# V of all heads made in the recurrent stage and kept in HBM, its splits on GpSimd, and the attention loop reordered

## The chip, the cores and the metric

The kernel runs on one core of a Trainium2 chip. The metric is device time in microseconds (us) from the first to the last instruction of one execution; lower is better. The core's engines each run their own queue of instructions in order and wait for one another through semaphores: TensorE (PE in the profile, PEld its weight loads), VectorE (DVE), ScalarE (ACT), GpSimd (POOL), and SyncE (SP), whose queue issues most of the transfers.

## What is computed

A GRU runs over 128 time steps of 16 sequences with 256 features; its output is added to `x`. A transformer block follows on 16 sequences of 128 tokens, with 16 heads of 128 and a conditioning vector per sequence. Cut to what matters here:

```python
x = x + gru(cond, x, W_ih, W_hh, b_ih, b_hh)          # 128 steps, one after the other
shift1, scale1, gate1, shift2, scale2, gate2 = split(cond @ ada_w + ada_b, 6)
x1 = layernorm(x) * (1 + scale1) + shift1
q, k, v = split(x1 @ qkv_w + qkv_b)                    # 16 heads of 128
p = softmax(q @ k.T / sqrt(128))
x = x + gate1 * ((p @ v) @ out_w + out_b)
x2 = layernorm(x) * (1 + scale2) + shift2
x = x + gate2 * (gelu(x2 @ ffn_w1 + ffn_b1) @ ffn_w2 + ffn_b2)
```

## The kernel before, in words

Products of float32 values are made of float16 halves: a value is split into a high half (a rounded copy) and a low half (value minus high half), and three matmuls, high by high, low by high and high by low, add up in PSUM (`product`, lines 428 to 430). Splitting a value therefore takes one copy (most on ScalarE) and one subtraction (most on VectorE).

The kernel has three stages.

*The recurrence.* 16 blocks (r) of 8 time steps (s). In a step TensorE multiplies the state with the gate weights (`gru_step`, lines 535 and 543), ScalarE and VectorE make the gates in turn, and a scan on VectorE (line 1210) makes the next state, for which the next step's matmuls wait. In TensorE's queue, behind the step's last gate matmuls, stands filler: the input products of the next block (`x_products`), the turn and normalisation of the rows of the block before (`rows_T`, `rows_back`), which gives y = x1 for 8 more tokens of all 16 sequences, and `ahead(item)`: q and k of the four heads 0, 6, 8, 14 (`AHEAD`), for all sequences, a block of 8 tokens at a time, kept on the chip as `qk_hi`, `qk_lo`. ScalarE also splits the weights, four pieces of 320 columns a block (`piece_high`, line 901), and GpSimd their low halves (line 347).

*Attention.* 64 head steps d: four groups g of four sequences, 16 heads each. In a step the kernel makes q and k of the head unless it is one of the four (`queries`, `keys`, 6 matmuls of 512 columns each), V of the head (`values`, 24 matmuls of 128 columns), the scores (`scores`, 12 of 128), the row maximum on VectorE (line 1282), four exponentials on ScalarE (line 996), the normalisation on VectorE (line 1299, counted by `s_pn`), the high half of p on ScalarE (`prob_high`, line 989, `p_h`), the low half on VectorE (`prob_low`, line 1293, `p_l`), two transposing transfers issued by SyncE (`turn`, line 307, `p_turn`), p times V (`attend`, 12 of 128) and the output projection (`project_out`, 6 of 512). The order of the work is written out by hand for each engine. On TensorE a step d is keys(d), values(d), project_out(d-3), attend(d-2), queries(d+1), scores(d). There is one buffer each of p, its halves and their transposes. At the end of a group GpSimd makes sums and low halves of the second normalisation (lines 378, 387, 393, 400), each behind the maximum of a given head (`behind_max`).

*Feed-forward.* 32 tiles (`up`, `down`) for the four groups, and the output.

Of the kernel before, what the change touches and what calls it, by code (L numbers as in the profile page):

```python
# [15 lines left out]
P = 128  # L16
# [23 lines left out]
QKV_PIECES = -(-3 * INNER * KD // PC)  # L40

HEADS = NG * H
AHEAD = (0, 6, 8, 14)
NA = len(AHEAD)
ITEMS = [(e, n, 1, 0, B, 4, 2 * P) for n in range(NBL - 2) for e in range(NA)]
LAST_ITEMS = {"old": (0, NBL - 2, 1, 0, B, 2, 0), "new": (0, NBL - 1, 1, 0, QUAD, 3, 0), 1: (1, NBL - 2, 2, 0, B, 5, 0),
              "rest": (0, NBL - 1, 1, QUAD, B, 4, 0), 2: (2, NBL - 2, 2, 0, B, 4, 0), 3: (3, NBL - 2, 2, 0, B, 4, 0)}
LAST = {what: len(ITEMS) + i for i, what in enumerate(LAST_ITEMS)}
ITEMS += LAST_ITEMS.values()
WHOLE = [d for d in range(HEADS) if d % H not in AHEAD]  # L50
SLOTS = [(which, head) for head in AHEAD for which in range(2)]
SLOTS += [(which, head) for which in range(3) for head in range(H) if (which, head) not in SLOTS]
AHEAD_PIECES = -(-2 * NA * KD * DH // PC)
LAG = 3
# [5 lines left out]
FORWARD, BACK, HIGH = {4: 0, 6: 1}, {11: 0, 12: 1}, {12: 0, 14: 1}  # L60
ROW_TILES = {3: (0, 0), 4: (0, 1), 5: (1, 0), 6: (1, 1)}
STATS, CENTRE, MODULATE = {6: 0, 8: 1}, {10: 0, 11: 1}, {12: 0, 14: 1}
VAR = 9
LATER = {4: "rest", 6: 2, 9: 3}
REST_AT, SUM_AT, LOW_AT = 5, 11, 15

AHEAD_PLACE = {0: 0, 2: 1, 4: 2, 6: 3}
# [13 lines left out]
def build(nc, x, cols_in, cond_rows, gate_rows, W_ih, W_hh, ada_a, ada_r, ada_b, weights, out):  # L81
# [3 lines left out]
    with ctx:  # L85
# [15 lines left out]
        y_hi = sb("y_hi", [P, KD, B, T], f16)  # L101
        y_lo = sb("y_lo", [P, KD, B, T], f16)
        qk_hi = sb("qk_hi", [P, NA, 2, B, T], f16)
        qk_lo = sb("qk_lo", [P, NA, 2, B, T], f16)
# [50 lines left out]
        v_hi = sb("v_hi", [P, 3, N], f16)  # L155
        v_lo = sb("v_lo", [P, 3, N], f16)
        pT_hi = sb("pT_hi", [P, QUAD, T], f16)
        pT_lo = sb("pT_lo", [P, QUAD, T], f16)
        aT_hi = sb("aT_hi", [P, 2, N], f16)
        aT_lo = sb("aT_lo", [P, 2, N], f16)  # L160
        prob = sb("prob", [P, QUAD, T])
        p_hi = sb("p_hi", [P, N], f16)
        p_lo = sb("p_lo", [P, N], f16)
        mx = sb("mx", [P, QUAD])
        nmx = sb("nmx", [P, QUAD])
        den = sb("den", [P, QUAD])
        rden = sb("rden", [P, QUAD])
        four = sb("four", [P, 4, N], f16)
# [7 lines left out]
        gated = xn[:, :, :].rearrange("p j d -> p (j d)").rearrange("p (k j t) -> p k j t", k=KD, j=QUAD)  # L176
        qT_hi, qT_lo, kT_hi, kT_lo = (four[:, i, :] for i in range(4))
        hid_hi, hid_lo = four[:, 0:2, :], four[:, 2:4, :]
# [14 lines left out]
        def sems(names):  # L193
# [15 lines left out]
        xt_hi, xt_lo, xp_lo, qk_mm, qk_h, qk_l = sems("xt_hi xt_lo xp_lo qk_mm qk_h qk_l")  # L209
# [3 lines left out]
        (ln_ag, ln_nat, ln_T, ln_st, ln_ve, ln_rstd, ln_xn, ln_B, ln_y, ln_hi, ln_lo) = sems(  # L213
            "ln_ag ln_nat ln_T ln_st ln_ve ln_rstd ln_xn ln_B ln_y ln_hi ln_lo")
        (q_mm, k_mm, v_mm, s_mm, a_mm, o_mm, q_h, k_h, v_h, q_l, k_l, v_l, s_mx, s_nm, s_exp, s_rd, s_pn,
         p_h, p_l, p_turn, a_h, a_l, o_gated, o_res) = sems(
             "q_mm k_mm v_mm s_mm a_mm o_mm q_h k_h v_h q_l k_l v_l s_mx s_nm s_exp s_rd s_pn "
             "p_h p_l p_turn a_h a_l o_gated o_res")
# [16 lines left out]
        flat_prob = prob[:, :, :].rearrange("p j t -> p (j t)")  # L235

        def ahead_place(item, part):

            e, n, blocks, b0, b1, at, col = ITEMS[item]
            width = blocks * BS * (b1 - b0)  # L240
            ps = bank[at][:, col + part * width:col + (part + 1) * width].rearrange("p (b t) -> p b t", b=b1 - b0)
            return ps, slice(b0, b1), slice(n * BS, (n + blocks) * BS)

        def a_late(d):

            return d < HEADS - 1 and (d % H in AHEAD or (d + 1) % H in AHEAD)

        def whole_before(d):

            return sum(w < d for w in WHOLE)  # L250

        def tall_bank(d, which):

            return bank[which + (6 if d == WHOLE[1] else 0)]

# [4 lines left out]
        def up_bank(t):  # L260
            return bank[(0, 1, 4, 2)[t] if t < 4 else 1 + t % 2]

# [4 lines left out]
        def _(sp):  # L267
# [17 lines left out]

            for r in range(NBL - 1):
# [22 lines left out]
            for d in range(HEADS):  # L309
                turn(d)  # L310
# [1165 lines left out]
```

## Time and profile before

| | |
|---|---|
| time, median of 3 runs | 753.85 us (753.35 to 753.98) |
| span of the profiled execution | 754.3 us |
| mean granted TensorE clock, share of 2.4 GHz | 0.988 |
| TensorE busy | 724.2 us (96%) |
| VectorE, ScalarE, GpSimd busy | 580.0, 488.7, 104.7 us |
| recurrence, to the last scan | 0 to 267.8 us |
| first score maximum, last score maximum | 274.9, 660.4 us |
| end | 754.3 us |

A row of the profile names a line of the kernel, the engine, the operation, the output and inputs by the program's names (L1299 DVE prob<-prob,rden is the normalisation in line 1299), shapes as partitions x elements, and times. The views used are the page (busy time, chain of waits, transfers), the busy time in stretches, the instructions of one line with shortest, median and longest duration, and the instructions in order of time. Matmul ends are modelled, so the distance from start to start is the rate.

### The profile page before, as it was taken

What the parts mean: (1) busy time and instruction counts of PE and PEld (TensorE: products, weight loads), DVE (VectorE), ACT (ScalarE), POOL (GpSimd) and SP (SyncE); (2) the same over time, 40 slices, a digit from 0 to 9 for tenths busy, and PEclk for the clock granted to TensorE, in tenths of its full rate; (3) what the DMA queues carried; (4) which work ended last, traced back from release to release, by engine and by line L of the source; (5) the groups of instructions that cost most, each with busy time, mean ns of one, the idle gap of its engine ahead of it and who ended that gap; (6) DMA issues with size and microseconds to landing.
All of it is one profiled execution on the core that took longest, in us unless ns stands there. A gap on an engine that the chain in (4) does not pass through costs nothing.

```text
span 754.3 us, 25863 instructions
## 1 busy us (share of the span) xinstructions
PE 724.2 (96%) x10644; PEld 534.1 (71%) x10644; DVE 580.0 (77%) x1625; ACT 488.7 (65%) x1665; POOL 104.7 (14%) x134
## 2 busy tenths in 40 slices
PE   6899999999999989999999999999999999999997
PEld 5688888888888766767667677676676766644554
DVE  5778877888888877777778888788887888834643
ACT  4456555665565566677777677777678777766453
POOL 0322222223232210000001011010110101000040
PEclk9899998999999999999999999999999999999999
DMA  6311121111121002222222312222222231310001
GB/s 234 102 45 45 46 69 63 45 46 44 46 62 55 3 16 43 44 43 42 46 43 43 50 37 56 38 50 44 44 43 43 43 49 37 48 25 28 29 1 56
DMA packets 77869, 36.75 MB, mean 49 GB/s; under 512 B 70539, under 2 KB 73783, under 8 KB 77751
## 3 DMA queue, kind: packets, MB, share of 16 engines
q1 hardware_dynamic: 77175, 33.52, 19.5%
q8 instruction: 84, 1.38, 0.7%
q10 hardware_dynamic: 576, 1.57, 0.6%
q14 instruction: 34, 0.28, 0.1%
HBM read 16.20 MB, written 2.10 MB: 24 GB/s over the span
## 4 chain that ended last, share of the span: by engine, by line
PE 83%; DVE 6%; DMA 4%; ACT 3%; issue 2%; SPq 2%; DVEq 0%; POOL 0%; POOLq 0%
PE bank L428 20%; PE bank L430 19%; PE bank L429 19%; PE bank L535 12%; PE bank L543 5%; PE bank L448 4%; DMA pT_lo<-p_lo 3%; DVE h_hi L1210 2%; SPq L307 2%; ACT zg L936 1%; DVE nu L1204 1%; PE bank L435 1%; PE bank L464 1%; PE bank L457 1%; DMA x<-in_x 0%
## 5 line engine op out<-in xcount | busy, mean ns | idle before, releaser
L428 PE MATMUL bank<-y_hi,w_hi 128*128 128x512 f16 (+2 forms) x496 | 140.6, 301 | 0.3 <-DVE qk_lo L1187 0.2
L430 PE MATMUL bank<-y_lo,w_hi 128*128 128x512 f16 (+2 forms) x496 | 140.8, 302 | 0.0
L429 PE MATMUL bank<-y_hi,w_lo 128*128 128x512 f16 (+2 forms) x496 | 140.7, 302 | 0.0
L535 PE MATMUL bank<-h_hi,whh_hi 128*128 128x16 f16 x1536 | 110.9, 173 | 14.1 <-DVE h_hi L1210 11.7
L535 PEld LDWEIGHTS bank<-h_hi,whh_hi 128*128 128x128 f16 x1536 | 89.5, 96 | 36.7 <-DVE h_hi L1210 34.5
L996 ACT ACTIVATE prob<-bank,nmx 128x128 f32<-128x128 f32 x256 | 90.4, 366 | 29.7 <-DVE nmx L1285 29.7
L535 PE MATMUL bank<-h_hi,whh_lo 128*128 128x16 f16 x1536 | 108.7, 172 | 0.0
L535 PEld LDWEIGHTS bank<-h_hi,whh_lo 128*128 128x128 f16 x1536 | 90.0, 96 | 0.1
L428 PE MATMUL bank<-w_hi,y_hi 128*128 128x128 f16 x512 | 89.1, 219 | 0.5 <-DVE v_lo L1289 0.5
L429 PE MATMUL bank<-w_hi,y_lo 128*128 128x128 f16 x512 | 89.1, 219 | 0.0
L430 PE MATMUL bank<-w_lo,y_hi 128*128 128x128 f16 x512 | 89.1, 219 | 0.0
L543 PE MATMUL bank<-h_lo,whh_hi 128*128 128x16 f16 x1536 | 77.6, 172 | 0.1
L347 POOL TENSOR_TENSOR w_lo<-stage,w_hi 128x320 f16<-128x320 f32 x64 | 52.2, 816 | 143.1 <-DVE h_lo L1215 141.1
L430 PEld LDWEIGHTS bank<-y_lo,w_hi 128*128 128x128 f16 x496 | 48.9, 99 | 29.4
L934 ACT ACTIVATE zr<-bank 128x32 f32<-128x32 f32 x128 | 25.6, 200 | 58.6 <-PE bank L543 55.2
L428 PEld LDWEIGHTS bank<-y_hi,w_hi 128*128 128x128 f16 x496 | 48.8, 98 | 19.6 <-issue 0.5
L429 PEld LDWEIGHTS bank<-y_hi,w_lo 128*128 128x128 f16 x496 | 48.8, 99 | 17.5
L989 ACT ACTIVATE p_hi<-prob 128x512 f16<-128x512 f32 x64 | 40.5, 632 | 30.5 <-DVE prob L1299 19.5
L1282 DVE TENSOR_REDUCE mx<-bank 128x4 f32<-128x512 f32 x64 | 44.1, 689 | 18.3 <-PE bank L430 17.8
L1326 DVE TENSOR_TENSOR four<-nat,four 128x512 f16<-128x512 f32 (+1 forms) x33 | 22.7, 689 | 44.8 <-ACT four L1032 44.7
L543 PEld LDWEIGHTS bank<-h_lo,whh_hi 128*128 128x128 f16 x1536 | 56.3, 96 | 0.2 <-DVE h_lo L1215 0.2
L912 ACT ACTIVATE qk_hi<-bank,small 128x128 f16<-128x128 f32 (+3 forms) x124 | 39.1, 367 | 26.4 <-PE bank L430 26.4
(156 smaller groups left out, 2161.6 us busy)
## 6 DMA issues: line engine op xcount, KB each, us to landing
stage<-in_weights SPq DMA_DIRECT2D x16, 640.0 KB, 3.9
x<-in_x SPq DMA_DIRECT2D x16, 128.0 KB, 3.8
out<-xr SPq DMA_DIRECT2D x3, 512.0 KB, 3.1
xr<-in_ada_r SPq DMA_DIRECT2D x1, 1024.0 KB, 7.6
pT_hi<-p_hi SPq DMA_TRANSPOSE x64, 2.4
pT_lo<-p_lo SPq DMA_TRANSPOSE x64, 2.5
xr<-in_W_ih ACTq DMA_DIRECT2D x2, 384.0 KB, 3.8
xr<-in_W_hh ACTq DMA_DIRECT2D x2, 384.0 KB, 5.8
```

The costliest lines, as they stand in the source:

```text
L347: gtt(w_lo[:, j * PC:(j + 1) * PC], stage[:, r % 2, i * PC:(i + 1) * PC], w_hi[:, j * PC:(j + 1) * PC], sub).then_inc(piece_lo, 1)
L428: mm(ps, w[0], a[0], start=start, stop=False, skip_group_check=True)
L429: mm(ps, w[1], a[0], start=False, stop=False, skip_group_check=True)
L430: return mm(ps, w[0], a[1], start=False, stop=stop, skip_group_check=True)
L448: nc.tensor.matmul(gate_cols(n, m), w[:, k, m * P:(m + 1) * P], a[:, n % 2, k, :], start=False, stop=False, skip_group_check=True)
L535: nc.tensor.matmul(out(m0 + m), half[:, k, (m0 + m) * P:(m0 + m + 1) * P], h_hi[:, k * B:(k + 1) * B, 1], start=False, stop=False, skip_gr ...
L543: mm = nc.tensor.matmul(out(m0 + m), whh_hi[:, k, (m0 + m) * P:(m0 + m + 1) * P], h_lo[:, k * B:(k + 1) * B], start=False, stop=k == KD - ...
L912: op = nc.scalar.activation(qk_hi[:, e, part, b, t], ps, ident_f, bias=bT[:, at:at + 1])
L934: nc.scalar.activation(zr[:, :, 1], r_cols[r % 2][:, s, :], ACT.Sigmoid).then_inc(r_ok, 1)
L989: nc.scalar.activation(p_hi[:, :], flat_prob, copy).then_inc(p_h, 1)
L996: op = nc.scalar.activation(prob[:, j, :], bank[3][:, j * T:(j + 1) * T], ACT.Exp, bias=nmx[:, j:j + 1], scale=SCALE, accum_out=den[:, j:j ...
L1282: nc.vector.reduce_max(mx[:, :], bank[3][:, :].rearrange("p (j s) -> p j s", j=QUAD), AX.X).then_inc(s_mx, 1)
```

## The change

V of all 16 heads and sequences is made in the recurrence. An item (n, pair) of `VITEMS` multiplies block n of the rows (128 rows: 16 sequences by 8 tokens) with the V weights of two heads: 6 matmuls of 256 columns. `VPLACE` puts 109 of the 128 items behind steps 14 to 127, one a step from step 35 on; 19 (`VTAIL` and up) follow in the tail of the recurrence and among the first three heads. ScalarE copies the items of the recurrence from PSUM, ScalarE and VectorE in turn the others, to `v_rows`; SyncE stores half blocks of 512 KB to `v_spill` in HBM and loads 256 KB a head (`load_values`) into `v_full`. The q and k items ahead and `values` are gone; every head makes q and k in its own step.

In attention GpSimd makes the low half of p, and both halves of V from `v_full`. `prob`, the halves of p, q and k and the transposes have two buffers. TensorE's step is keys(d), project_out(d-4), queries(d+1), attend(d-2), scores(d). GpSimd's loop over heads carries its group-end work too. The second normalisation writes to space in the weight tiles (`x2_hi`, `x2_lo`), and its turns use the two banks of the projection. The diff, cut to its core:

```diff
+LAG = 4
+GATE, RESIDUAL = {4: 0, 6: 1}, {5: 0, 7: 1}
+STATS, CENTRE, MODULATE = {8: 0, 9: 1}, {11: 0, 12: 1}, {13: 0, 14: 1}
+VAR = 10
+REST, SUM, LOW = {9: 0, 10: 1}, {12: 0, 13: 1}, {0: 0, 1: 1}
...
             def turn(d):
                 for half_ok, src, dst in ((p_h, p_hi, pT_hi), (p_l, p_lo, pT_lo)):
                     sp.wait_ge(half_ok, d + 1)
-                    if d > 0:
-                        sp.wait_ge(a_mm, d)
-                    sp.dma_start_transpose(dst[:, :, :], src[:, :]).then_inc(p_turn, 16)
+                    if d > 1:
+                        sp.wait_ge(a_mm, d - 1)
+                    sp.dma_start_transpose(dst[:, d % 2, :, :], src[:, d % 2, :]).then_inc(p_turn[d % 2], 16)
+            def load_values(d):
+                g, head = d // H, d % H
+                if d > 1:
+                    sp.wait_ge(v_l, d - 1)
+                sp.dma_start(v_full[:, d % 2, :].rearrange("p (j c) -> p j c", j=QUAD),
+                             v_spill[:, g * QUAD:(g + 1) * QUAD, head * DH:(head + 1) * DH]).then_inc(v_in[d % 2], 16)
+            for n in (NBL - 2, NBL - 1):
+                sp.wait_ge(v_out[n % 2][0], 16 * (NBL // 2))
+            load_values(0)
+            load_values(1)
+            turn(0)
+            for d in range(1, HEADS):
                 turn(d)
...
+                if d + 1 < HEADS:
+                    load_values(d + 1)
...
-            for g in range(NG - 1):
-                first = (g + 1) * H
-                for k in range(KD):
-                    behind_max(first + REST_AT + k)
-                    bias_rest(g, k)
...
+            def prob_low(d):
+                pool.wait_ge(p_h, d + 1)
+                gtt(p_lo[:, d % 2, :], flat_prob[d % 2], p_hi[:, d % 2, :], sub).then_inc(p_l, 1)
+            def value_split(d):
+                pool.wait_ge(v_in[d % 2], 16 * (d // 2 + 1))
+                if d > 2:
+                    pool.wait_ge(a_mm, d - 2)
+                nc.gpsimd.tensor_copy(v_hi[:, d % 3, :], v_full[:, d % 2, :]).then_inc(v_h, 1)
+                pool.wait_ge(v_h, d + 1)
+                gtt(v_lo[:, d % 3, :], v_full[:, d % 2, :], v_hi[:, d % 3, :], sub).then_inc(v_l, 1)
+            for d in range(HEADS):
+                prob_low(d)
+                if d >= H and (d + 1) % H == VAR:
+                    norm_rstd(d // H - 1)
+                value_split(d)
+                g, i = (d + 2) // H, (d + 2) % H
+                if d + 2 < HEADS:
+                    pool.wait_ge(s_pn, d + 3)
+                if g > 0 and i in REST:
+                    bias_rest(g - 1, REST[i])
+                if g > 0 and i in SUM:
+                    sum_rest(g - 1, SUM[i])
+                if g > 1 and i in LOW:
+                    norm_low(g - 2, LOW[i])
...
+            def value_item(i):
+                n, pair = VITEMS[i]
+                pe.wait_ge(lb_lo, n + 1)
...
+                for k in range(KD):
+                    mm = product(ps, (y_hi[:, k, n, :], y_lo[:, k, n, :]),
+                                 (wq_hi[:, heads, k, :], wq_lo[:, heads, k, :]), k == 0, k == KD - 1)
+                mm.then_inc(v_mm, 1)
...
-            share = (0, 0, 7, 9, 22, 25, 31, 32, 36)
+            share = (0, 0, 2, 9, 16, 23, 27, 33, 36)
...
+                    if t1 - 1 in VPLACE:
+                        value_item(VPLACE[t1 - 1])
...
             def attend(d):
-                pe.wait_ge(p_turn, 32 * (d + 1))
+                pe.wait_ge(p_turn[d % 2], 32 * (d // 2 + 1))
+                pe.wait_ge(v_l, d + 1)
...
+            for d in range(LAG, HEADS):
                 g, i = d // H, d % H
+                keys(d)
+                project_out(d - LAG)
...
+                if d < HEADS - 1:
+                    queries(d + 1)
...
+                attend(d - 2)
                 scores(d)
...
             def softmax(d):
                 act.wait_ge(s_nm, d + 1)
-                if d > 0:
-                    act.wait_ge(p_l, d)
+                if d > 1:
+                    act.wait_ge(p_l, d - 1)
...
+                    if t1 - 1 in VPLACE:
+                        value_out(VPLACE[t1 - 1])
...
+                softmax(d - 1)
+                key_high(d)
                 prob_high(d - 1)
...
+                    query_high(d + 1)
                 attend_high(d - 2)
...
                 score_max(d - 1)
...
+                query_low(d)
+                attend_low(d - 3)
+                softmax(d - 1)
+                key_low(d)
```

(The last two runs of lines are the loops over heads of ScalarE and VectorE.)

## Rows read from the trace of the kernel before

**Rows 1.** The page's chain that ended last: share of the span by engine.
```profile
PE 83%; DVE 6%; DMA 4%; ACT 3%; issue 2%; SPq 2%; DVEq 0%; POOL 0%; POOLq 0%
```
**Rows 2.** Busy time in stretches: stretch, length, busy us of each engine, granted clock, DMA.
```profile
core 0: us, PE busy (x) PEld busy (x) DVE busy (x) ACT busy (x) POOL busy (x), PEclk, DMA share, GB/s
12.00:267.80 255.80, 241.29 (x5951) 210.59 (x5951) 208.88 (x872) 145.34 (x722) 69.15 (x92) 0.97 0.18 57
293.10:660.40 367.30, 364.47 (x3851) 255.44 (x3850) 303.12 (x592) 269.54 (x792) 22.72 (x20) 1.00 0.25 44
```
**Rows 3.** One line, the scan that ends a step: duration, first and last start.
```profile
L1210 DVE TENSOR_TENSOR_SCAN h_hi<-zz,nu x128: 291/292/293, 12.0 to 267.6; 128x64 f16<-128x64 f32 x128
```
**Rows 4.** In order of time, TensorE in one step: start, duration, instruction.
```profile
264.81 0.25 PE L543 MATMUL bank<-h_lo,whh_hi 128*128 128x16 f16 x4
...
265.94 0.18 PE L535 MATMUL bank<-h_hi,whh_hi 128*128 128x16 f16 x1
```
**Rows 5.** In order of time, ScalarE in the same step.
```profile
265.26 0.23 ACT L939 ACTIVATE nu<-npre 128x32 f32<-128x32 f32 x1
...
266.65 0.20 ACT L934 ACTIVATE zr<-bank 128x32 f32<-128x32 f32 x1
```
**Rows 6.** In order of time, TensorE: matmuls of 256 columns back to back.
```profile
276.07 0.27 PE L428 MATMUL bank<-y_hi,w_hi 128*128 128x256 f16 x1
276.18 0.27 PE L429 MATMUL bank<-y_hi,w_lo 128*128 128x256 f16 x1
```
**Rows 7.** In order of time, TensorE: first of 24 narrow matmuls, then two of 512.
```profile
359.14 0.23 PE L428 MATMUL bank<-pT_hi,v_hi 128*128 128x128 f16 x1 [0.24 <-DMA pT_lo<-p_lo]
...
360.49 0.38 PE L428 MATMUL bank<-y_hi,w_hi 128*128 128x512 f16 x1
360.70 0.38 PE L429 MATMUL bank<-y_hi,w_lo 128*128 128x512 f16 x1
```
**Rows 8.** Instructions grouped by form: busy us, mean ns, idle before.
```profile
L901 ACT ACTIVATE w_hi<-stage 128x320 f16<-128x320 f32 x64 | 28.4, 469 | 0.0
```
**Rows 9.** The page's transfers: issuing queue, count, size, us to landing.
```profile
out<-xr SPq DMA_DIRECT2D x3, 512.0 KB, 3.1
```
**Rows 10.** In order of time, VectorE: maxima of heads 3, 14, 63, normalisation of 3.
```profile
293.14 0.68 DVE L1282 TENSOR_REDUCE mx<-bank 128x4 f32<-128x512 f32 x1
...
295.81 0.69 DVE L1299 TENSOR_TENSOR prob<-prob,rden 128x512 f32<-128x512 f32 x1
...
360.69 0.69 DVE L1282 TENSOR_REDUCE mx<-bank 128x4 f32<-128x512 f32 x1 [0.16 <-PE bank L430]
...
660.40 0.69 DVE L1282 TENSOR_REDUCE mx<-bank 128x4 f32<-128x512 f32 x1 [0.35 <-PE bank L430]
```
**Rows 11.** In order of time: an operation on VectorE that releases one on GpSimd.
```profile
399.31 0.17 DVE L1285 TENSOR_SCALAR nmx<-mx 128x4 f32<-128x4 f32 x1
...
399.56 1.04 POOL L393 TENSOR_TENSOR xr<-xr,gb 128x512 f32<-128x512 f32 x1 [126.27 <-DVE nmx L1285]
```
**Rows 12.** Single lines, GpSimd's 512-column operations: shortest, median, longest ns.
```profile
L387 POOL TENSOR_TENSOR y_lo<-xn,y_hi x8: 1154/1158/1164, 459.3 to 723.8; 128x512 f16<-128x512 f32 x8
...
L393 POOL TENSOR_TENSOR xr<-xr,gb x8: 1037/1040/1487, 399.6 to 726.4; 128x512 f32<-128x512 f32 x8
...
L400 POOL TENSOR_TENSOR xr<-xr x8: 1256/1268/1758, 434.7 to 729.1; 128x512 f32<-128x512 f32 x8
```
**Rows 13.** In order of time: a high half of p and the issue of its transpose.
```profile
302.91 0.63 ACT L989 ACTIVATE p_hi<-prob 128x512 f16<-128x512 f32 x1 [0.40 <-DVE prob L1299]
...
303.77 1.19 SPq L307 DMA_TRANSPOSE pT_hi<-p_hi  x1
```
**Rows 14.** In order of time: low transpose, attend's first weight load; landing times.
```profile
356.62 1.22 SPq L307 DMA_TRANSPOSE pT_lo<-p_lo  x1
...
359.13 0.10 PEld L428 LDWEIGHTS bank<-pT_hi,v_hi 128*128 128x128 f16 x1 [0.73 <-DMA pT_lo<-p_lo]
...
DMA to landing us min/median/max: 2.4/2.5/4.2
```
**Rows 15.** Busy time in stretches, the end of the kernel; columns as in rows 2.
```profile
749.00:750.00 1.00, 0.92 (x7) 0.50 (x6) 0.89 (x5) 0.00 (x0) 0.00 (x0) 1.00 0.00 0
...
753.00:754.00 1.00, 0.00 (x0) 0.00 (x0) 0.00 (x0) 0.00 (x0) 0.00 (x0) 0.67 0.43 125
```

More of the change, by code:

```diff
@@ L39, with value_items, by_scalar, taken @@
 GK = 32 + 2 * GM
-QKV_PIECES = -(-3 * INNER * KD // PC)
+TALL_PIECES = -(-(H + 2) * DH * KD // PC)
 HEADS = NG * H
[L43 to L54, printed above, removed]
+PAIRS = H // 2
+VP = 2 * DH
+SIDE = INNER // 2
+SLOTS = [(2, head) for head in range(H)] + [(which, head) for head in range(H) for which in range(2)]
+def value_items():
+    first = [(0, 0), (0, 1), (0, 2), (0, 3), (0, 4), None, None, None, (1, 0), (1, 1), (0, 5), (1, 2), (1, 3),
+             (0, 6), None, None, (0, 7), (1, 4), (1, 5), (1, 6), (1, 7)]
+    order, place = [], {}
+    for i, item in enumerate(first):
+        if item:
+            place[BS + 6 + i] = len(order)
+            order.append(item)
+    at = BS + 6 + len(first)
+    for n in range(2, NBL - 2):
+        for pair in range(PAIRS):
+            if at < T:
+                place[at] = len(order)
+                at += 1
+            order.append((n, pair))
+    order += [(NBL - 2, pair) for pair in range(PAIRS // 2)] + [(NBL - 1, pair) for pair in range(PAIRS // 2)]
+    order += [(NBL - 2, pair) for pair in range(PAIRS // 2, PAIRS)]
+    order += [(NBL - 1, pair) for pair in range(PAIRS // 2, PAIRS)]
+    return order, place
+VITEMS, VPLACE = value_items()
+VTAIL = len(VPLACE)
+def by_scalar(i):
+    return i < VTAIL or i % 2 == 0
+def taken(i):
+    scalar = sum(by_scalar(j) for j in range(i + 1))
+    return scalar, i + 1 - scalar
+def piece_of(pair):
+    return -(-(pair + 1) * VP * KD // PC)
+LAG = 4
 TILES = NG * FM
@@ L154, in build @@
         xn = sb("xn", [P, QUAD, D])
[L155 to L168, printed above, removed]
+        gated = sb("gated", [P, KD, QUAD, T])
+        hid_hi = sb("hid_hi", [P, 2, N], f16)
+        hid_lo = sb("hid_lo", [P, 2, N], f16)
+        v_spill = nc.dram_tensor("v_spill", (T, B, INNER), f32).ap()
         bank = [ctx.enter_context(nc.psum_tensor(f"bank{i}", [P, 512], f32)) for i in range(8)]
@@ L800, in last_down @@
                     mm.then_inc(f_down, 1)
[L802 to L804 removed]
+            for which, ready in ((0, q_mm), (1, k_mm)):
+                if which == 0:
+                    pe.wait_ge(lb_lo, NBL)
+                tall_parts(tall_rest, 0, which, last).then_inc(ready, 1)
+            tall_parts(tall_rest, 1, 1, before)
+            tall_parts(tall_rest, 1, 0, last).then_inc(q_mm, 1)
+            tall_parts(tall_rest, 1, 1, last).then_inc(k_mm, 1)
+            for i in range(VTAIL + 5, VTAIL + 7):
+                value_item(i)
             scores(0)
[L806 to L807 removed]
+            for i in range(VTAIL + 7, VTAIL + 11):
+                value_item(i)
+            pe.wait_ge(piece_lo, NBL * PB)
+            queries(2)
             scores(1)
[L809 to L811 removed]
+            value_item(VTAIL + 11)
+            value_item(VTAIL + 12)
+            keys(2)
+            value_item(VTAIL + 13)
+            value_item(VTAIL + 14)
             queries(3)
```

557 lines of the change are left out of this document (233 added, 324 removed).

## The prediction

> **What bounds the kernel now.** I read the chain that ended last first: TensorE carries 83% of it [rows 1]. An average over stages says little, so the second view is the busy time by stage [rows 2]. From 293.1 to 660.4 us, the 60 head steps between the score maxima of heads 3 and 63, TensorE is busy for 364.5 of 367.3 us: there attention runs at the rate of its matmuls. In the recurrence (12.0 to 267.8 us) it is busy for 241 of 256 us, but the third view, the 128 scans that end the steps, shows another limit [rows 3]: 127 intervals in 255.6 us, 2.01 us each, 1.96 us wherever the clock is full. In one such step [rows 4] the last gate matmuls start at 264.81, and the next step's first matmul at 265.94 begins only when the scan has ended; the matmuls between are filler of no weight while they fit. Four 25 ns matmuls after 264.81 leave a window of about 1.02 us. ScalarE has such a window too [rows 5]: its tanh ends at 265.49, the next gate is due at 266.65.
>
> **The change: the recurrence.** Removed are 56 items of q and k ahead, each 12 matmuls of 128 columns; added are 109 items of V, one a step from step 35 on, each 6 matmuls of 256 columns. At 0.11 us from start to start [rows 6] an item takes 0.65 us. With the gate products of the next block, up to 7 matmuls of about 0.056 us (24 narrow matmuls in 1.35 us [rows 7]), a step's filler is 1.04 us: just at the window's edge. At s = 1, where the bias matmul lies too (1,024 columns, some 0.45 us), it is over by about 0.2. ScalarE has more to lose. The V copy can start only when the item's last matmul is through (264.92 + 0.65 + 0.2 = 265.8) and takes about 0.37 us, 256/320 of the 0.469 us of a weight piece [rows 8]; until 266.65 there is then room for one piece. At s = 3 there are two: over by 0.45 us. At s = 7 a modulation tile and a piece: over by 0.15 in eight rounds. Some 14 x 0.45 + 12 x 0.2 + 8 x 0.15 = 10 us; VectorE drops a 0.34 us operation a step, and the steps beyond 1.96 us (6.7 us in all [rows 3]) may be fewer with more columns in TensorE. I take **+8**, bounds -6 (nothing late, no slow step) and +22.
>
> **Between the stages.** 19 items of V remain for the tail. Eleven of them (7 us of TensorE) stand before the second query product; five before the last rows are turned or the first scores. The start of head 0 comes about 3 us later. Then attend(0) needs V back from HBM: the eleventh item is copied after the softmax of head 0, stored (512 KB landed in 3.1 us [rows 9]), loaded (256 KB in 512-byte pieces; I take 4 us, no transfer like it is here; 2 to 6), split on GpSimd (about 2.5 us, below). That is some 4 us after TensorE could start it, of which the queue's work behind it hides nothing. **+7** at head 3, bounds 0 and +12.
>
> **Attention, the matmuls.** V's 24 matmuls leave; per head remain 24 of 128 columns (1.35 us) and 18 of 512 (0.215 each [rows 7], 3.87): 5.22 us, where a head now takes 367.3 / 60 = 6.12 on the mean. If TensorE stayed the limit, 60 heads would take 313 us, 54 us less. VectorE loses two operations a head, ScalarE one. What is decisive is what attend waits for.
>
> **Attention, the new wait.** GpSimd's loop over heads now does prob_low(d), value_split(d), and then, for every d, waits for s_pn >= d + 3. s_pn counts the normalisations on VectorE, so this is softmax(d+2). Queued behind it is prob_low(d+1). So the low half of head d+1 is made only after the softmax of head d+2, although its own high half has been ready for a whole head. On TensorE the order is keys(d+3), project_out, queries(d+4), attend(d+1), scores(d+3): attend(d+1) needs that low half transposed. Scores(d+2) -> softmax(d+2) -> prob_low(d+1) -> transpose -> attend(d+1) -> scores(d+3) is thus a closed loop that advances one head. Its length, from one score maximum to the next:
> - maximum to end of the normalisation: 293.14 to 295.81 + 0.69 = 3.36 us [rows 10]. Two VectorE splits stand beside the exponentials in it, as they do now.
> - hand-over to GpSimd: 0.08 us [rows 11].
> - prob_low on GpSimd, 128x512, f16 from f32 and f16: 1.16 us, the row of the same form [rows 12] (other forms 1.04 and 1.27). It was 0.69 us on VectorE.
> - to the queue: 0.23 us, end of p_hi at 303.54 to the issue at 303.77 [rows 13].
> - issue of the low transpose to attend's first weight load: 356.62 to 359.13, 2.51 us [rows 14]. Landing takes 2.4 us at least, 2.5 in the middle and 4.2 at most, where it follows the high half's closely. Here the high half goes out a head earlier, so 2.5.
> - attend and scores to the next maximum: 359.13 to 360.69, 1.56 us [rows 10, 14].
>
> Sum **8.90 us a head**. TensorE's other work between, three products of 1.29 us, fills 3.87 of the 7.34 us before attend: it idles for about 3.5 us a head. v_l stays inside: cast and subtraction follow prob_low. The trace has no 512-column cast on GpSimd; it costs between nothing and the 1.16 us of the subtraction, which reads two inputs where the cast reads one. Even at the upper end 1.16 + 1.16 + 0.2 = 2.5 us is under the 2.74 us of queue and transpose, so either value adds nothing. The load of V is asked for a head earlier, behind the low transpose, and has 8.9 us. GpSimd's other work sits between the wait and prob_low, so it lengthens the loop: in the 16 heads with such an operation 6 x 1.04 + 6 x 1.27 + 4 x 1.16 = 18 us [rows 12]. The four-row transposes and the norm's VectorE work fall in the idle time. 60 x 8.90 + 18 = 552 us, against 367.3 [rows 10]: **+185**. Bounds: 8.5 us a head (shorter hand-overs) gives +161; 9.2 (the transpose at 2.8) +203.
>
> A row bears on prob_low's price: its sibling forms have 1.04 and 1.27 us as medians but 1.49 and 1.76 at most [rows 12], and the slow ones ran in the last stage, beside a VectorE subtraction of two SBUF tensors. The Trainium skill (GPSIMD Engine Reference, Key points) says that GpSimd shares its SBUF interfaces with VectorE and contends with VectorE instructions that have two SBUF inputs. By that rule the new wait does good, as it keeps GpSimd away from the normalisation; were prob_low hit all the same, the sum would be 0.45 x 60 = 27 us more.
>
> **The clock.** At the end of the kernel the last matmul is over at 749.9 and the granted clock falls from 2.4 to 1.2 GHz within 753 to 754 (mean 0.67 [rows 15]), so about 3.4 us later. It also fell for parts of the recurrence (mean 0.97 [rows 2]), where TensorE was busy but with narrow matmuls. [...] The three products have slack at half speed; attend and scores have not: up to 24 x 0.056 = 1.35 us a head, 0 to +80 us. A half-speed product shortens the next gap, so it can't happen everywhere at will: I take **+25**, a third.
>
> **The end.** One more project_out follows the last scores (+1.3), and attend(62) stands in the same loop with three products before it: 7.34 - 3.87 = +3.5. Together **+5**. Feed-forward is the same.
>
> **How the numbers follow.** 754.3 + 8 + 7 + 185 + 25 + 5 = 984; the profiled span is 0.4 us above the median of the runs, so **984 us**. The range goes from 754.3 - 6 + 0 + 161 + 0 + 5 = 914 to 754.3 + 15 + 12 + 203 + 80 + 5 = 1069; the ends need all terms on one side, so 920 to 1060.
>
> **Rivals.**
> - The loop isn't closed, attention stays at the rate of its matmuls. If prob_low(d) waited only for its own high half, the chain to attend would be 3.36 + 0.7 (p_hi, 0.63 [rows 13], and its hand-over) + 1.16 + 0.23 + 2.51 = 8.0 us, and TensorE's work between scores(d) and attend(d) is 5.22 + 3.87 = 9.1: it would be hidden. Then 754.3 + 8 + 7 - 54 + 1 = **716 us**, faster. It decides at one point: whether s_pn can reach d + 3 before the scores of head d + 2. I find no second place that counts it up. Chance 0.05.
> - The clock is at 1.2 GHz in every attend: 8.90 + 1.35 = 10.25 us a head, 984 - 25 + 80 = **1039 us**. [...] Against: after each gap 5.2 us of dense matmuls. Chance 0.15.
> - GpSimd runs beside VectorE's two-input operations after all: +27, **1011 us**. Chance 0.08.
> - Forecast 0.7; 0.02 for the loop shorter than 8.5 us.
>
> A measurement of this kernel can tell 0.2% from no change. Faster 0.05, same 0.01, slower 0.94.
>
> **What would show it.** Right: from head 3 on score maxima about 8.9 us apart, TensorE idle for 3 to 3.5 us before attend with the low transpose as releaser, GpSimd's prob_low(d+1) released by the normalisation of head d+2, and steps of 10 us where GpSimd has a norm operation. The recurrence ends 8 us later, with gates late at s = 3. Wrong: maxima 5.2 us apart, or prob_low released by p_hi; steps far over 2.1 us in the recurrence; v_l or the load of V as attend's releaser; a granted clock that stays at 1.0 or at 0.5 in attention.

## The result and the profile after

The changed kernel takes **994.73 us** in the median of four runs (991.13 to 1000.12), against 753.91 before: a ratio of 1.3194, interval [1.3148, 1.324]. It is 32% slower. The profiled execution took 991.13 us, with a span of 989.3 us.

The page's chain that ended last, the share of the span by engine, answers to [rows 1]:

```profile
issue 39%; PE 35%; POOL 20%; DVE 2%; DMA 2%; ACT 1%; SPq 0%; POOLq 0%; DVEq 0%
```

Before, TensorE carried 83% of the chain. Now it carries 35%; a fifth is GpSimd, and 39% is time for which the view finds no releaser. The busy time in stretches answers to [rows 2] and has its columns: the recurrence, the start of attention, the 60 head steps between the score maxima of heads 3 and 63, and the end.

```profile
12.00:280.30 268.30, 260.80 (x5921) 233.75 (x5921) 181.89 (x761) 151.20 (x718) 69.12 (x92) 0.97 0.36 105
280.30:314.00 33.70, 28.27 (x271) 20.74 (x270) 18.04 (x44) 18.88 (x52) 7.12 (x8) 0.99 0.41 102
314.00:889.30 575.30, 405.63 (x2569) 231.87 (x2568) 259.17 (x501) 256.08 (x749) 194.11 (x199) 0.86 0.27 57
889.30:989.30 100.00, 92.18 (x490) 47.28 (x488) 43.25 (x99) 51.35 (x90) 17.47 (x15) 0.98 0.09 28
```

In the third stretch TensorE was busy for 364.5 of 367.3 us; now it is busy for 405.6 of 575.3, with fewer matmuls and at a granted clock of 0.86 in place of 1.00. That stretch holds 208 of the 235 us by which the span grew. By the same four marks in both traces (last scan, maximum of head 3, maximum of head 63, end):

| us | before | after | difference | predicted |
|---|---|---|---|---|
| to the last scan | 267.55 | 280.06 | +12.5 | +8 |
| from there to the maximum of head 3 | 25.59 | 33.97 | +8.4 | +7 |
| heads 3 to 63 | 367.26 | 575.28 | +208.0 | +210 (185 + 25 for the clock) |
| from there to the end | 93.9 | 100.0 | +6.1 | +5 |

The waits, the engine and operation, what it waited for, us in total, times, longest:

```profile
DVE mx L1319 <- PE bank L527: 293.3, 63, 7.0
POOL p_lo L487 <- DVE prob L1328: 285.7, 46, 7.0
PEld bank L525 <- DMA pT_lo<-p_lo: 208.2, 63, 4.9
```

These three are the closed loop that the prediction describes: the maximum waits for the scores, GpSimd's low half of p waits for a normalisation, attend waits for the transposed low half. One turn of it in order of time, from one score maximum to the next (start, duration, instruction):

```profile
607.15 0.69 DVE L1319 TENSOR_REDUCE mx<-bank 128x4 f32<-128x512 f32 x1 [6.92 <-PE bank L527]
...
609.83 0.69 DVE L1328 TENSOR_TENSOR prob<-prob,rden 128x512 f32<-128x512 f32 x1
...
610.60 1.16 POOL L487 TENSOR_TENSOR p_lo<-prob,p_hi 128x512 f16<-128x512 f32 x1 [6.90 <-DVE prob L1328]
...
611.78 1.19 SPq L373 DMA_TRANSPOSE pT_lo<-p_lo  x1
...
614.27 0.10 PEld L525 LDWEIGHTS bank<-pT_hi,v_hi 128*128 128x128 f16 x1 [2.23 <-DMA pT_lo<-p_lo]
...
615.82 0.69 DVE L1319 TENSOR_REDUCE mx<-bank 128x4 f32<-128x512 f32 x1 [4.64 <-PE bank L527]
```

Every link has its row: 3.37 us from the maximum to the end of the normalisation (610.52), 0.08 to GpSimd, 1.18 for p_lo and the queue, 2.49 from the issue of the transpose to attend's first weight load, 1.55 for attend and scores. That is 8.67 us, and undisturbed heads are 8.62 to 8.70 us apart all through the stage. The mean is 9.59; the rest is heads with a norm operation and heads in which the clock fell (the run with the idle time filled tells the two apart). A fall of the clock can be seen in the distance of two matmuls of 512 columns, 0.22 us at 2.4 GHz and 0.43 us at 1.2 GHz (the granted clock from 624.6 to 626.0 us is 0.50):

```profile
610.42 0.38 PE L525 MATMUL bank<-aT_hi,w_hi 128*128 128x512 f16 x1
...
610.64 0.38 PE L526 MATMUL bank<-aT_hi,w_lo 128*128 128x512 f16 x1
...
624.73 0.63 PE L525 MATMUL bank<-y_hi,w_hi 128*128 128x512 f16 x1
625.16 0.63 PE L526 MATMUL bank<-y_hi,w_lo 128*128 128x512 f16 x1
```

### The profile page after: what moved, and what is told of

Same layout as the page of the kernel before. It is cut to its first block, busy times and chain, and to the rows that moved or that the text cites. A ratio compares the mean times of both kernels' runs of the same rounds, so it can differ in the third digit from the quotient of the medians.

```text
span 989.3 us, 23647 instructions
## 1 busy us (share of the span) xinstructions
PE 793.4 (80%) x9324; PEld 539.1 (54%) x9324; DVE 508.3 (51%) x1423; ACT 483.5 (49%) x1621; POOL 289.5 (29%) x326
## 4 chain that ended last, share of the span: by engine, by line
issue 39%; PE 35%; POOL 20%; DVE 2%; DMA 2%; ACT 1%; SPq 0%; POOLq 0%; DVEq 0%
PE bank L630 8%; POOL p_lo L487 7%; POOL v_lo L496 7%; PE bank L525 6%; PE bank L527 5%; PE bank L526 5%; PE bank L545 4%; PE bank L638 4%; POOL v_hi L494 3%; DMA pT_lo<-p_lo 1%; POOL xr L482 1%; PE bank L532 1%; DVE h_hi L1249 1%; POOL xr L475 1%; PE bank L597 1%
## 5 line engine op out<-in xcount | busy, mean ns | idle before, releaser
L525 PE MATMUL bank<-pT_hi,v_hi 128*128 128x128 f16 x256 | 57.1, 250 | 177.7 <-DMA pT_lo<-p_lo 177.7
L487 POOL TENSOR_TENSOR p_lo<-prob,p_hi 128x512 f16<-128x512 f32 x64 | 74.1, 1157 | 294.1 <-DVE prob L1328 285.7
L525 PE MATMUL bank<-y_hi,w_hi 128*128 128x512 f16 x248 | 111.9, 451 | 0.0
L526 PE MATMUL bank<-y_hi,w_lo 128*128 128x512 f16 x248 | 109.5, 441 | 0.0
L527 PE MATMUL bank<-y_lo,w_hi 128*128 128x512 f16 x248 | 107.3, 433 | 0.0
L496 POOL TENSOR_TENSOR v_lo<-v_full,v_hi 128x512 f16<-128x512 f32 x64 | 74.5, 1165 | 5.1
L525 PE MATMUL bank<-w_hi,y_hi 128*128 128x256 f16 x256 | 69.6, 272 | 0.7 <-DVE v_rows L1228 0.4
L527 PE MATMUL bank<-w_lo,y_hi 128*128 128x256 f16 x256 | 69.9, 273 | 0.0
L526 PE MATMUL bank<-w_hi,y_lo 128*128 128x256 f16 x256 | 69.8, 273 | 0.0
L527 PE MATMUL bank<-four 128*128 128x128 f16 x256 | 66.0, 274 | 0.0
L526 PE MATMUL bank<-four 128*128 128x128 f16 x256 | 65.3, 272 | 0.0
```

Source lines behind the costliest of these rows:

```text
L487: gtt(p_lo[:, d % 2, :], flat_prob[d % 2], p_hi[:, d % 2, :], sub).then_inc(p_l, 1)
L496: gtt(v_lo[:, d % 3, :], v_full[:, d % 2, :], v_hi[:, d % 3, :], sub).then_inc(v_l, 1)
L525: mm(ps, w[0], a[0], start=start, stop=False, skip_group_check=True)
L526: mm(ps, w[1], a[0], start=False, stop=False, skip_group_check=True)
L527: return mm(ps, w[0], a[1], start=False, stop=stop, skip_group_check=True)
```

## The experiments

Eight kernels were run. All start from the changed kernel or from an experiment on it; ratios are to the kernel before, measured in the same series.

### The wait taken away

```diff
-                if d + 2 < HEADS:
-                    pool.wait_ge(s_pn, d + 3)
```

> The changed kernel without GpSimd's wait for s_pn >= d + 3; nothing else differs. Closed loop (the wait sets 8.7 us a head, the rest is the clock and GpSimd's norm work): the low half of head d+1 then follows its own high half, the chain to attend (about 8.0 us) fits in the 9.1 us that TensorE needs from scores to attend, and the score maxima come 5.2 to 5.4 us apart: 60 x 5.3 = 318 us in place of 575, granted clock near 1.0, total 725 to 740 us. Rival (GpSimd as such: 2.9 us of splits a head with three operations in a row, or V's way through HBM, sets the pace): maxima stay above 7 us apart, total above 840 us.

Measured: **750.94 us**, ratio 0.9964 [0.9948, 0.9979]. The wait is the cause of the loss: without it 244 us go, and the stretch from head 3 to head 63 takes 342.0 us in place of 575.3. But the stretch does not come down to the rate of its matmuls (313 us), and the time lies between what the two theories gave: where GpSimd has no norm operation, most heads are 5.22 and 5.97 us apart in turn. The order of time of VectorE and GpSimd shows what the slower ones have. The negated maximum `nmx`, four elements a partition, takes 0.17 us in 33 of the 60 heads, more than 1 us in 25 and 0.44 and 0.55 us in two:

```profile
493.76 0.17 DVE L1320 TENSOR_SCALAR nmx<-mx 128x4 f32<-128x4 f32 x1
...
493.93 1.16 POOL L496 TENSOR_TENSOR v_lo<-v_full,v_hi 128x512 f16<-128x512 f32 x1
...
498.94 1.15 POOL L496 TENSOR_TENSOR v_lo<-v_full,v_hi 128x512 f16<-128x512 f32 x1
...
498.99 1.13 DVE L1320 TENSOR_SCALAR nmx<-mx 128x4 f32<-128x4 f32 x1
```

In the first head `nmx` starts 0.17 us ahead of `v_lo` and takes its 0.17. In the second it starts 0.05 behind `v_lo` and ends at 500.12, just behind `v_lo`'s end at 500.09. In each of the 27 heads in which `nmx` is longer than 0.17 us, it ends 0.02 to 0.03 us behind the end of a GpSimd operation (`v_lo`, once `v_hi`). All exponentials, and with them the whole chain, wait for `nmx`. Whether the meeting is the cause or a coincidence was left to the next run.

### The wait taken away, and v_lo begun behind the maximum

On top of the edit above:

```diff
                 pool.wait_ge(v_h, d + 1)
+                if d + 1 < HEADS:
+                    pool.wait_ge(s_nm, d + 2)
                 gtt(v_lo[:, d % 3, :], v_full[:, d % 2, :], v_hi[:, d % 3, :], sub).then_inc(v_l, 1)
```

> The edit of e1_no_wait (GpSimd's wait for the normalisation taken away) and one more: GpSimd begins the subtraction that makes v_lo(d) only when VectorE has made nmx(d+1), so that v_lo can no longer run beside that small operation. In e1_no_wait every second nmx met v_lo and took 1.09 to 1.13 us in place of 0.17, and the maxima were alternately 5.22 and 5.97 us apart (342 us from head 3 to head 63, span 750.1). If it is the meeting with GpSimd that stretches nmx, nmx is 0.17 in every head, the maxima are 5.2 to 5.4 us apart, heads 3 to 63 take 315 to 325 us and the kernel 722 to 736 us, under both kernels. If the meeting is a coincidence and something else sets the second interval, or if the waiting GpSimd is late with p_lo, the time stays at 745 us or more.

Measured: **735.4 us** (735.34 to 736.65), ratio 0.9724 [0.97, 0.9747]: 2.8% faster than the kernel before, and 259 us faster than the change as it was made. One line of each trace, VectorE's `nmx` in attention (count, busy us, mean ns, idle before), first in the experiment above:

```profile
L1320 DVE TENSOR_SCALAR nmx<-mx 128x4 f32<-128x4 f32 x60 | 34.7, 579 | 2.0
```

and in this one:

```profile
L1322 DVE TENSOR_SCALAR nmx<-mx 128x4 f32<-128x4 f32 x60 | 10.2, 170 | 2.0
```

The busy time of this kernel in attention, with the columns of [rows 2]:

```profile
313.00:638.00 325.00, 321.54 (x2560) 190.76 (x2558) 260.39 (x501) 243.17 (x748) 194.48 (x198) 1.00 0.46 100
```

The `nmx` is 0.17 us in every head, 24.5 us of busy time are gone, and heads 3 to 63 take 325.7 us where they took 342.0. So it was the meeting with GpSimd. TensorE is busy for 321.5 of 325.0 us at a granted clock of 1.00: attention runs close to its matmuls' rate, 26 of the 60 heads 5.21 to 5.24 us apart. The Trainium skill (SBUF — State Buffer, section "SBUF: two separate sides") says that VectorE and GpSimd share a port pair as an exclusive lock, and that, between a GpSimd operation and a VectorE operation that has two SBUF inputs or runs in a mode with two ports, whichever starts first holds the pair for its whole length while the other blocks. These rows agree with the lock: the one that came 0.05 us later waited for the other's end. `nmx` has one SBUF input; that it runs in such a mode is shown by no run here.

### Scores ahead of attend, the wait kept

```diff
                     pe.wait_ge(q_l, HEADS)
                     up(0)
-                attend(d - 2)
                 scores(d)
+                attend(d - 2)
```

(This is the loop over heads from 4 on; at head 3 the order stays attend, then scores.)

> The changed kernel with the wait kept, but scores(d) issued before attend(d-2) in TensorE's loop. Closed loop: scores(d+3) then no longer stands behind attend(d+1), so the loop scores(d+2), softmax(d+2), prob_low(d+1), transpose, attend(d+1), scores(d+4) advances two heads in about 7.2 + 0.7 + 3.9 + 0.7 = 12.5 us: 6.2 to 6.7 us a head, 60 heads in 375 to 420 us with GpSimd's norm work, total 790 to 840 us. Rival (the wait itself is harmless, some resource takes 8.7 us a head: GpSimd, the transposes, the clock): the order doesn't matter, total stays within 2% of 991 us.

Measured: **918.17 us**, ratio 1.217 [1.2136, 1.2203]. Neither theory: the order matters, but heads are still 8.3 us apart in the mean. In order of time, GpSimd, VectorE, TensorE and ScalarE:

```profile
353.69 1.15 POOL L496 TENSOR_TENSOR v_lo<-v_full,v_hi 128x512 f16<-128x512 f32 x1
...
354.18 0.69 DVE L1322 TENSOR_SCALAR nmx<-mx 128x4 f32<-128x4 f32 x1
...
355.54 0.23 PE L525 MATMUL bank<-pT_hi,v_hi 128*128 128x128 f16 x1 [2.12 <-DMA pT_lo<-p_lo]
...
356.42 0.69 ACT L1067 ACTIVATE aT_hi<-bank,small 128x512 f16<-128x512 f32 x1 [3.05 <-PE bank L527]
357.00 0.36 ACT L1047 ACTIVATE prob<-bank,nmx 128x128 f32<-128x128 f32 x1
```

The scores' negated maximum is ready at 354.87 (`nmx` met `v_lo` here too and took 0.69 us), but the exponentials start at 357.00, for ahead of them in ScalarE's queue stands the copy of an attend (`aT_hi`), which waits for that attend, which waits for its transposed low half. The loop had been opened on TensorE and was closed again one engine further on.

### The same, and the copies of attend one head later

On top of the edit above, ScalarE copies attend(d-3) in place of attend(d-2) at step d, and VectorE does its part behind the normalisation:

```diff
-                attend_high(d - 2)
+                attend_high(d - 3)
...
-                attend_low(d - 3)
                 softmax(d - 1)
                 key_low(d)
+                attend_low(d - 3)
```

> The edit of e3_scores_first (scores(d) before attend(d-2), GpSimd's wait kept; 918.17 us, maxima 8.3 us apart in the mean) and one more: the two copies of an attend out of its bank go one head later, ScalarE's behind the exponentials and p_hi of head d-1, VectorE's behind the normalisation of head d-1. My reading of e3_scores_first is that its loop was closed again through the in-order queues, because the exponentials of head d+3 stood on ScalarE behind the copy of attend(d+1). If that is so, the loop now goes on by two heads a turn: a turn of 8.7 to 9.9 us plus scores of 1.6 us, 5.2 to 6.2 us a head, with GpSimd's wait itself still there: heads 3 to 63 take 330 to 400 us and the kernel 745 to 820 us. If the copies were not what closed it, it stays at 900 us or more.

Measured: **891.02 us**, ratio 1.1781 [1.1748, 1.1814]. Over 745 to 820, so the size was missed; heads are 6.95 us apart where nothing disturbs them and 7.9 in the mean. The loop does now advance two heads a turn, as expected. But I had counted too little in a turn:

```profile
353.18 0.68 DVE L1319 TENSOR_REDUCE mx<-bank 128x4 f32<-128x512 f32 x1
...
355.85 0.69 DVE L1328 TENSOR_TENSOR prob<-prob,rden 128x512 f32<-128x512 f32 x1
...
356.62 1.16 POOL L487 TENSOR_TENSOR p_lo<-prob,p_hi 128x512 f16<-128x512 f32 x1 [4.00 <-DVE prob L1328]
...
357.81 1.19 SPq L373 DMA_TRANSPOSE pT_lo<-p_lo  x1
...
360.37 0.22 PE L525 MATMUL bank<-pT_hi,v_hi 128*128 128x128 f16 x1 [1.56 <-DMA pT_lo<-p_lo]
...
364.92 0.22 PE L525 MATMUL bank<-four 128*128 128x128 f16 x1
...
366.42 0.75 DVE L1343 SCALAR_TENSOR_TENSOR aT_lo<-bank,small,aT_hi 128x512 f16<-128x512 f32 x1 [2.26 <-ACT aT_hi L1067]
367.08 0.68 DVE L1319 TENSOR_REDUCE mx<-bank 128x4 f32<-128x512 f32 x1
```

Between attend (360.37) and the scores that come behind it (364.92) now lie the three products of a head, 3.9 us that were outside the loop before; and the maximum (367.08) stands on VectorE behind `aT_lo`, which waits for its high half, 1.3 us after the scores' end. The turn from the maximum at 353.18 to the one at 367.08, two heads on, is 3.36 us to the end of the normalisation, 0.08, 1.19 to the issue of the transpose, 2.56 to attend, 4.55 to the scores and 2.16 to the maximum. These 13.9 us for two heads are 6.95 a head. The wait keeps some loop closed in the two other orders that I tried; of the kernels run here, only those without it are free of it.

### The idle time filled with matmuls

In attention TensorE makes the product queries(d+1) three times; nothing waits for the copies, which overwrite one another.

```diff
-                for k in range(KD):
+                for k in list(range(KD)) * (3 if which == 0 and LAG < d < HEADS else 1):
```

> The changed kernel with the product of queries(d+1) done three times over in TensorE's loop (the first two results are overwritten with the same values): 2.6 us more matmuls a head, in the time in which TensorE idles before attend. If the falls of the granted clock cost what they seem to (maxima 9.59 apart on the mean where undisturbed ones are 8.66 apart), the clock stays near 1.0 and the heads take 8.66 plus GpSimd's norm work: 60 x 8.66 + 18 = 538 in place of 575 us, total 950 to 960 us, less time for more work. If the clock is not what lengthens them, or the idle time was not free: 991 us or more.

Measured: **959.51 us**, ratio 1.2725 [1.2689, 1.2761]: 35 us less with 12 more matmuls of 512 columns in nearly each head. The stretch from head 3 to head 63:

```profile
316.50:860.40 543.90, 485.28 (x3278) 258.73 (x3277) 259.12 (x502) 255.58 (x749) 194.10 (x199) 0.99 0.26 61
```

The granted clock is 0.99 in place of 0.86, and the stretch takes 543.9 us in place of 575.3. So the falls of the clock cost 31.4 us of attention. The matmuls of attend and scores, which have no slack, bear this out: in the changed kernel 16 of 60 attends and 28 of 60 scores run wholly at the lower clock, 0.104 to 0.107 us from start to start in place of 0.056, and others in part, which adds up to 33 us; with the idle time filled it is 2 us. What remains is the loop, 60 x 8.66 = 519.6 us, and 24.3 us more, of which these 2 us are the clock's and the rest lies in the heads with norm operations.

### One matmul of V in place of six

```diff
                 n, pair = VITEMS[i]
...
+                if i < VTAIL:
+                    mm = nc.tensor.matmul(ps, y_hi[:, 0, n, :], wq_hi[:, heads, 0, :], start=True, stop=True,
+                                          skip_group_check=True)
```

(and the six left out for these items)

> The changed kernel with five of the six matmuls of each V item in the recurrence left out (V is incomplete; copies, stores, loads and waits stay). If TensorE's filler is what makes the recurrence later (mean step 2.11 against 1.96 us): every step at 1.96 to 1.98 us, the last scan 10 to 13 us earlier, total 975 to 985 us. If ScalarE's copies and weight pieces are (the +0.45 us at s = 3 of the prediction): the steps stay near 2.11 us, total within 3 us of 991.

Measured: 988.09 us, ratio 1.3107, over the 975 to 985 expected. The last scan starts at 270.88, 9.2 us earlier than in the changed kernel, somewhat under the 10 to 13 expected. The recurrence in stretches:

```profile
12.00:270.90 258.90, 234.80 (x5414) 194.20 (x5411) 182.00 (x762) 140.24 (x722) 68.94 (x92) 0.82 0.38 110
```

ScalarE's copies, VectorE's work and the stores are all still there, so their number is not what lengthens the steps. But a copy can also start earlier when its item has one matmul, so this run alone does not tell TensorE's lateness from ScalarE's; the starts of the next step's first matmul do, and they are given below with the prediction. The granted clock is 0.82 where it was 0.97, and fourteen steps from the second round on took 2.2 to 2.7 us, at a granted clock of 0.50 to 0.79: V also gave TensorE the work that kept its clock up. Heads 3 to 63 took 579.9 us, 4.6 more; that says nothing, for in the two runs below, with the same attention, they took 578.9 and 577.0.

### The order of the input products

Which matmuls are late is told apart by moving them. The steps of a round in the changed kernel are 1.96 us long in the median, except those behind s = 1 (2.31), s = 3 (2.05), s = 5 (2.20), s = 6 (2.21) and, with a modulation tile, s = 7 (2.25).

```diff
-            products = [(m, k, i) for m in range(GM) for k in range(KD) for i in range(3)]
+            products = [(m, k, i) for m in (4, 5, 0, 1, 2, 3) for k in range(KD) for i in range(3)]
```

> The changed kernel with the input products of a round made in another order: those of the n gate (twelve of 36, 0.107 us each in the trace of the changed kernel, the others 0.056) come first, so they fall into the steps s = 2 and 3 in place of s = 5, 6 and 7; nothing else moves. If it is their pace that makes TensorE late in s = 6 (filler of 0.65 for V + 6 x 0.107 against some 1.02 us of room), the step after s = 6 loses its 0.24 us and is like a step without lateness (1.95 to 2.0 us), the steps after s = 2 and s = 3 become 0.3 to 0.4 us longer, and the last scan of the recurrence starts at 279 to 284 us (changed kernel 280.06). If it is ScalarE's evictions or the loads of those steps, the steps after s = 5, 6 and 7 stay as they are and those after s = 2 and 3 too.

Measured: the lateness moved with the products. Behind s = 1, 2, 3, 5 and 6 the steps are 2.42, 2.32, 2.11, 2.04 and 1.96 us long; the last scan starts at 281.29 (one run, span 996.8 us). The sum stays, as expected; the step behind s = 3 grew by 0.06 us only and not by the 0.3 to 0.4 expected, for just three of the twelve products fall there (seven in s = 2, two in s = 1). In s = 2 seven of the n gate's products stand behind V's; TensorE, in order of time:

```profile
237.73 0.32 PE L545 MATMUL bank<-xb_hi,wih_lo 128*128 128x128 f16 x1
237.84 0.31 PE L545 MATMUL bank<-xb_lo,wih_hi 128*128 128x128 f16 x1
```

They are 0.11 us apart, where the products of the other gates are 0.056 apart at the same clock.

### The n gate's products into adjacent columns

The n gate keeps its two parts in one PSUM bank with their columns alternating, so a product writes 16 columns two apart. Here it writes 16 adjacent ones, and the gate no longer finds its sums where it reads them:

```diff
-                return (r_cols[n % 2][:, :, c], z_cols[n % 2][:, :, c], n_cols[n % 2][:, :, c, 1])[m // 2]
+                n_flat = n_bank[n % 2][:, :].rearrange("p (t j) -> p t j", t=BS)
+                return (r_cols[n % 2][:, :, c], z_cols[n % 2][:, :, c], n_flat[:, :, c])[m // 2]
```

> The changed kernel, in which the input products of the n gate go to 16 adjacent PSUM columns a time step in place of 16 columns two apart (the columns are the wrong ones for the gate, so this kernel's recurrence computes something else; its instructions, their count and their shapes stay). If the two-column stride is what makes these twelve products of a round 0.107 us each in place of 0.056, they come down to 0.056, the lateness behind s = 6 and s = 7 goes (2.20 and 1.97 to 2.25 us to 1.96 to 2.1) and that behind s = 5 shrinks (2.20 to about 2.05), and the last scan starts at 271 to 275 us (changed kernel 280.06); the kernel takes 982 to 992 us. If it is the n gate's weights, or the bank, and not the stride, the products stay at 0.107 us and the last scan at 279 us or later.

Measured: 989.55 us (989.09 to 994.74), ratio 1.3098; the last scan starts at 275.16, at the edge of what was expected. The products of an s = 6, in order of time:

```profile
224.19 0.22 PE L546 MATMUL bank<-xb_hi,wih_hi 128*128 128x128 f16 x1
...
224.41 0.22 PE L546 MATMUL bank<-xb_hi,wih_lo 128*128 128x128 f16 x1
224.47 0.22 PE L546 MATMUL bank<-xb_lo,wih_hi 128*128 128x128 f16 x1
```

They come 0.05 to 0.06 us apart, and the next is the first matmul of the following step (224.57). The steps behind s = 5 and 6 are 2.04 and 1.96 us. So the stride of two in the written columns is the cause, not the n gate's weights and not its bank. The order of the computation needs the alternating columns (one scan reads both parts in turn), so this kernel shows the price alone; it leaves out the right sums of the gate.

## Why the prediction was right, and where a step of it failed

The forecast was 984 us (920 to 1060); the profiled execution took 991.13 and the median is 994.73. By its steps:

**The new wait and the closed loop: right.** Mechanism, place and price: 8.90 us a head were forecast, 8.62 to 8.70 are what undisturbed heads take. Against the parts of the sum only one was mis-sized: from the start of p_lo to the issue of its transpose it took 1.18 us and not 1.16 + 0.23; the 0.23 us were an issue behind ScalarE [rows 13], and SyncE was at once there behind GpSimd. The transpose (2.49 against 2.51 [rows 14]), attend and scores (1.55 against 1.56) and the normalisation (3.37 against 3.36 [rows 10]) held. The whole difference hung on one line, and the run without it shows that.

**GpSimd's other operations in the loop: somewhat small.** 18 us were forecast from the operations' durations [rows 12]; with the idle time filled the heads take 24.3 us more than the loop, some 22 of them in heads with norm work. I didn't divide the difference of 4 to 6 us.

**The clock: right in kind, a little small.** +25 was taken as a third of the way to the upper bound, and for the third no row stood; the run with filled idle time gives 31.4 us in attention. The price was put where it fell, on attend and scores. Before attend TensorE idles 1.5 to 4.5 us, 2.8 in the median, where some 3.5 were forecast. The rival with the lower clock in every attend (1039 us) did not come: 33 of 60 attends ran wholly at 2.4 GHz. The two terms above and this one err in opposite directions: 60 x (8.66 - 8.90) = -14, +6 and +6, so that attention as a whole came out at +208.0 against +210. The precise agreement of that row is luck in part.

**Between the stages and the end: right.** The first score maximum comes 3.8 us later behind the last scan (forecast 3) and head 3's another 4.6 us later (forecast 4). The load of V, for which no row stood, lands in 2.9 us (I took 4), the store in 3.8 where the row taken for it had 3.1 [rows 9]. The end is +6.1 against +5.

**The recurrence: the sum near, the reason mostly wrong.** +12.5 against +8, within its bounds. The step that failed is "ScalarE has more to lose". At s = 3, with two weight pieces, I expected 0.45 us; the step behind it is 0.09 us over 1.96. VectorE's scan, ScalarE and the first matmul behind the scan, in order of time:

```profile
238.44 0.29 DVE L1249 TENSOR_TENSOR_SCAN h_hi<-zz,nu 128x64 f16<-128x64 f32 x1
...
238.60 0.39 ACT L971 ACTIVATE v_rows<-bank 128x256 f32<-128x256 f32 x1 [0.27 <-PE bank L527]
...
238.79 0.17 PE L630 MATMUL bank<-h_hi,whh_hi 128*128 128x16 f16 x1
...
238.88 0.82 ACT L961 ACTIVATE w_hi<-stage 128x320 f16<-128x320 f32 x2
...
239.60 0.19 ACT L992 ACTIVATE zr<-bank 128x32 f32<-128x32 f32 x1
```

Two pieces end 0.82 us after the first starts, not 2 x 0.469 [rows 8], and the next operation starts even before that: ScalarE's operations overlap, and their durations can't be added up. At s = 3 the first matmul does start on time, 0.06 us behind the scan's end, and the gate `zr` 0.81 us behind it where 0.70 is usual: these 0.1 us are ScalarE's. Everywhere else the lateness is TensorE's: behind s = 1, 5, 6 and 7 the first matmul starts 0.43, 0.27, 0.29 and 0.32 us behind the scan's end in the median in place of 0.06, and the gate follows it as usual. The term that was mis-sized is "up to 7 matmuls of about 0.056 us": it was read from the matmuls of attention [rows 7] and put on the input products, of which those of the n gate take twice that. An s = 6 in the changed kernel, TensorE and the scans:

```profile
244.60 0.27 PE L545 MATMUL bank<-xb_hi,wih_hi 128*128 128x128 f16 x1
...
244.64 0.29 DVE L1249 TENSOR_TENSOR_SCAN h_hi<-zz,nu 128x64 f16<-128x64 f32 x1
...
245.00 0.31 PE L545 MATMUL bank<-xb_hi,wih_lo 128*128 128x128 f16 x1
245.10 0.31 PE L545 MATMUL bank<-xb_lo,wih_hi 128*128 128x128 f16 x1
245.21 0.21 PE L630 MATMUL bank<-h_hi,whh_hi 128*128 128x16 f16 x1
...
246.84 0.29 DVE L1249 TENSOR_TENSOR_SCAN h_hi<-zz,nu 128x64 f16<-128x64 f32 x1
```

The scan ends at 244.93, but the next step's first matmul can start at 245.21 only, behind six products 0.109 us apart (0.107 in the expectations is this figure read too low): 0.65 + 6 x 0.109 = 1.30 us of filler in a window of 1.02. The same products ran at 0.109 us in the trace of the kernel before, where the price could have been read:

```profile
231.95 0.31 PE L448 MATMUL bank<-xb_hi,wih_hi 128*128 128x128 f16 x1
232.06 0.31 PE L448 MATMUL bank<-xb_hi,wih_lo 128*128 128x128 f16 x1
```

The bias matmul at s = 1 was priced right in kind (0.35 measured, 0.2 forecast).

**A slip in the range.** Its upper end was added up with +15 for the recurrence, whose own bound is +22; with that the sum is 1076 and not 1069.

**The rivals.** "The loop isn't closed" was given 716 us. With the wait away the kernel takes 750.94: the recurrence accounts for 4.5 us of the difference, and attention, 342.0 us against the 313 of its matmuls, for 29. The prediction had weighed the contention of GpSimd and VectorE only as a stretch of GpSimd's p_lo (+27 us in the third rival). In the changed kernel p_lo is 1149 to 1169 ns in all 64 heads, so that rival did not occur; and where the two do meet, it is not the normalisation but a VectorE operation of 0.17 us that pays, and it is on the chain. As the prediction said, the new wait does keep GpSimd away from VectorE's chain. That is worth 16 us (heads 3 to 63, 342.0 less 325.7) and costs 244; a wait for the maximum in place of the wait for the normalisation gets the one without the other.

**What stays open.** In the fastest kernel heads 3 to 63 take 325.7 us, 12.5 over 60 x 5.22; the slower intervals, 5.4 to 6.1 us, are heads with norm operations (and one of 6.25 us at head 4, which has none), and what sets each was not tried. Nor was a layout for the n gate that keeps both the scan and the adjacent columns.

## What to carry to other kernels

A wait that only keeps work in order can close a loop through all the others: follow it round from the counted event back to itself, and count in each queue what stands ahead of the next link; the sum of the links is the time of a turn, and the number of heads by which it advances divides it. Opening such a loop on one engine helps only in part while another in-order queue closes it; here two reorderings gave back 77 and 104 of the 244 us that taking the wait away gave. Take the price of a matmul from its own line, not from another of the same shape: the spacing of the columns that it writes belongs to its price.

## What the runs showed of the hardware

- A product of 128 columns into PSUM columns two apart comes every 0.109 us, into adjacent columns every 0.056, at a full granted clock.
- A VectorE operation on four elements a partition takes 0.17 us alone and up to 1.16 us when a GpSimd operation on 512 columns has just started; in all 27 heads of the run without the wait in which it was longer, it ended 0.02 to 0.03 us behind such an operation.
- More matmuls can mean less time: with 12 more of 512 columns in nearly each head, 35 us less, since the granted clock in attention is 0.99 in place of 0.86. In the recurrence, fewer matmuls lowered it from 0.97 to 0.82.
- On GpSimd a cast of 512 columns from f32 to f16 takes 0.61 us, about half of a subtraction of that width (1.16).
